# Attention parts made by GpSimd in the loop and five tiles projected in its last slots, in a two-layer transformer kernel

## The reference, cut to what matters

```
ada = silu(c) @ W_ada + b_ada                       # six rows: shift, scale, gate, twice
h = layernorm(x) * (1 + scale_msa) + shift_msa
qkv = h @ W_qkv + b_qkv                             # 16 heads of 18
o = softmax(q k^T / sqrt(18)) v                     # over 1024 tokens of each of 2 sequences
x = x + gate_msa * (o @ W_proj + b_proj)
h = layernorm(x) * (1 + scale_mlp) + shift_mlp
x = x + gate_mlp * (gelu(h @ W_fc1 + b_fc1) @ W_fc2 + b_fc2)
```

## Time and profile before

| what | us |
|---|---|
| median of 3 runs | 917.32 |
| lowest and highest | 916.29, 917.46 |
| the profiled execution | 916.52 |
| its span in the trace | 914.4 |

### The profile page before, as it was taken

One profiled execution on the slowest core, in us unless ns is written; L12 is line 12 of the kernel. 1 busy time (PEld: TensorE's weight loads), 2 busy tenths in 40 slices (PEclk: granted clock), 3 DMA queues, 4 the chain that ended last, 5 costly groups with the idle time before them and its releaser, 6 DMA issues. The chain is left out here.

```text
span 914.4 us, 16701 instructions
## 1 busy us (share of the span) xinstructions
PE 792.0 (87%) x6096; PEld 365.0 (40%) x6096; DVE 649.9 (71%) x1273; ACT 533.5 (58%) x751; POOL 269.9 (30%) x347
## 2 busy tenths in 40 slices
PE   1568989999988989898878899999979875999996
PEld 0334222222222222222215465566646553666564
DVE  4849788888888898989707856646687798844521
ACT  4433576777676777767885636536547634546630
POOL 4320110214463411010005426341223456421122
PEclk9979799999999999999999899999989996999999
DMA  7202000110112110000040011011676720000000
GB/s 227 69 21 72 20 27 27 28 47 20 40 34 59 34 34 14 22 19 20 2 108 0 11 40 41 1 38 44 156 177 163 173 52 16 12 8 27 26 27 27
DMA packets 52127, 45.35 MB, mean 50 GB/s; under 512 B 23898, under 2 KB 41236, under 8 KB 52055
## 3 DMA queue, kind: packets, MB, share of 16 engines
q1 hardware_dynamic: 47613, 36.35, 15.3%
q10 hardware_dynamic: 4442, 8.04, 2.8%
HBM read 27.66 MB, written 9.46 MB: 41 GB/s over the span
## 5 line engine op out<-in xcount | busy, mean ns | idle before, releaser
L921 DVE TENSOR_REDUCE row_max<-ps 128x1 f32<-128x512 f32 x512 | 322.3, 683 | 60.3 <-PE ps L1653 59.4
L1413 ACT ACTIVATE probs<-ps 128x1024 f32<-128x1024 f32 x256 | 248.5, 1018 | 53.9 <-PE ps L1680 53.2
L1653 PE MATMUL ps<-stack_area 54*128 54x512 f16 x512 | 150.2, 388 | 27.1 <-DVE row_max L921 21.8
L1692 PE MATMUL ps<-probs,mlp_area 128*32 128x512 f32 x1024 | 137.2, 608 | 0.4 <-ACT probs L1413 0.4
L1680 PE MATMUL ps<-stack_area 56*128 56x512 f16 x512 | 110.1, 384 | 9.6 <-ACT probs L1413 9.3
L1653 PEld LDWEIGHTS ps<-stack_area 54*128 54x128 f16 x512 | 37.0, 93 | 191.5 <-DVE row_max L921 175.8
L1782 PE MATMUL ps<-mlp_area,w_fc 128*128 128x512 f16 x504 | 110.8, 379 | 1.7 <-issue 0.9
L1803 PE MATMUL ps<-w_fc,mlp_area 128*128 128x288 f16 x864 | 107.7, 286 | 4.6 <-DVE mlp_area L1061 4.6
L1454 ACT ACTIVATE mlp_area<-ps 128x512 f32<-128x512 f32 x72 | 42.9, 595 | 97.7 <-PE ps L1782 95.4
L1803 PEld LDWEIGHTS ps<-w_fc,mlp_area 128*128 128x128 f16 x864 | 83.8, 98 | 27.3 <-DVE mlp_area L1061 3.9
L738 POOL TENSOR_SCALAR neg_scaled<-neg_max 128x16 f32<-128x16 f32 x16 | 4.1, 254 | 292.8 <-DVE neg_max L928 292.8
(11 more groups left out here) (163 smaller groups left out, 1108.7 us busy)
## 6 DMA issues: line engine op xcount, KB each, us to landing
stack_area<-tokens SPq DMA_DIRECT2D x124, 36.0 KB
qkv_rows<-part_area ACTq DMA_DIRECT2D x14, 252.0 KB
qkv_rows<-probs ACTq DMA_DIRECT2D x10, 252.0 KB
x_sb<-in_x SPq DMA_DIRECT2D x4, 576.0 KB, 7.3
w_raw<-in_L_cond_W_fc SPq DMA_DIRECT2D x4, 576.0 KB
tokens<-qkv_rows SPq DMA_DIRECT2D x64, 36.0 KB
v_sb<-qkv_rows SPq DMA_DIRECT2D x16, 144.0 KB
w_raw<-in_L_cond_fc_w SPq DMA_DIRECT2D x4, 576.0 KB
```

Source lines behind the costliest of these rows:

```text
L921: nc.vector.reduce_max(row_max[:, p % 2, t, j, half:half + 1], bank(bk), AX.X).then_inc(max_done, 1)
L1413: nc.scalar.activation(probs[:, n % 2, 2 * c:2 * c + 2, :].rearrange("p h n -> p (h n)"), ps[:, 2 + 2 * c:4 + 2 * c, :].rearrange("p b n - ...
L1653: nc.tensor.matmul(bank(bk), stacks[rows, p % RING, 0, t * P:(t + 1) * P], stacks[rows, p % RING, 1, half * 512:(half + 1) * 512], start=T ...
L1692: mm = nc.tensor.matmul(bank(6)[at:at + VW, :], v_pad[:, TB * (p // BPAIR) + n, 2 * (p % BPAIR) + j, :], probs[:, n % 2, 2 * c + j, :], st ...
```

## The change

- POOL splits the result of each pair in the loop: `normalise_o` writes the pair into one of two float32 buffers (`o_flat`), and `split_attended(p-1)`, which stands behind `split_maxima(p+1)` and ahead of `split_weights`, makes the high part (a float16 copy) and the low part (a subtraction) in `att_parts`, the memory of `v_sb`. The factor 16 is now in the values (`take_v`). The last pair is split by ACT (`last_high`) and DVE (`last_low`) after the loop.
- Tiles 0 to 4 (all of the first sequence) are projected in slots 118 to 127: in an even slot PE turns a tile into bank 0 (`turn_attended`) and DVE copies the columns (`early_columns`), in the next slot PE multiplies into bank 1 (`proj_mms`) and DVE takes the projection. Both PE steps stand between the two halves of `scores`. DVE also makes the statistics of tiles 0 to 2 there. `turn_o` of pair 14 now has bank 7.
- After the loop tiles 5 to 15 follow. Their parts exist already, so that the steps L1442 and L1003 are gone. Tiles 5 to 7 don't need the last pair. The first four MLP tiles are normalised in the steps of tiles 6, 8, 10 and 12, and no longer in the last four.
- POOL's additions and reciprocal roots are unrolled, the roots made for two tiles at once (`invert_two`).
- SP waits for all tiles to be turned, where it waited for the low parts.

```diff
@@ memory
+        att_parts = v_sb[:].rearrange("p t h d -> p t (h d)").bitcast(F16).rearrange("p t (s n) -> p t s n", s=2)
+        o_flat = [tail[:, 2 * L + L // 2 + 2 * C // 2 * i:2 * L + L // 2 + C * (i + 1)] for i in range(2)]
+        freed_cols = tokens[:, 3 * 6 * C:5 * B * L // 2 + 5 * C]
+        hT_att = [freed_cols[:, 320 * i:320 * (i + 1)].bitcast(F16).rearrange("p (k n) -> p k n", k=5) for i in range(2)]
+        y_att = freed_cols[:, 640:640 + 2 * C].rearrange("p (a n) -> p a n", a=2)
@@ constants
+        TAIL_TILES = 5
+        TAIL_FROM = NPAIR * SLOTS - 2 * TAIL_TILES
+        MLP_AT = {6: 0, 8: 1, 10: 2, 12: 3}
@@ SP
-            sp.wait_ge(lo_ready[1], NT)
+            sp.wait_ge(turned[1], NT)
@@ POOL
+            def split_attended(p):
+                pool.wait_ge(o_ready, p + 1)
+                nc.gpsimd.tensor_copy(pair_parts(p, 0), pair_values(p)).then_inc(att_high, 1)
+                pool.wait_ge(att_high, p + 1)
+                nc.gpsimd.tensor_tensor(pair_parts(p, 1), pair_values(p), pair_parts(p, 0), ALU.subtract
+                                        ).then_inc(att_split, 1)
                         if p + 1 < NPAIR:
                             split_maxima(p + 1)
+                        if p:
+                            split_attended(p - 1)
                         if 0 <= p - FIRST_JOB < NJ - QKV_JOBS:
                             split_weights(0, ...)
-                    add_projection(0, 0)
-                    add_projection(0, 1)
-                    with pool.Fori(2, NT) as t:
-                        add_projection(0, t)
-                        invert(t - 2, NT + t - 2)
+                    for t in range(0, NT + 4, 2):
+                        if t < NT:
+                            add_projection(0, t)
+                            add_projection(0, t + 1)
+                        if t > 3:
+                            invert_two(t - 4, NT + t - 4)
@@ DVE, normalise_o
+                if p > 1:
+                    dve.wait_ge(att_split, p - 1)
-                nc.vector.tensor_tensor(v_sb[:, t0:t0 + TB, h:h + 2, 0:D], o[:, :, :, 0:D],
+                nc.vector.tensor_tensor(pair_values(p).rearrange("p t (j d) -> p t j d", j=2), o[:, :, :, 0:D],
@@ DVE, attention, at the end of slot s
+                    if s >= TAIL_FROM:
+                        t, late = divmod(s - TAIL_FROM, 2)
+                        if late:
+                            take_projection(0, t, t % 2, t < 2)
+                        else:
+                            if t > 1:
+                                first_mid_statistics(t - 2)
+                            if t == 0:
+                                dve.wait_ge(late_in, 16 * B)
+                            early_columns(t)
                 normalise_o(NPAIR - 1, 7)
+                last_low()
@@ DVE, after the loop
+                    for t in range(TAIL_TILES, NT + 4):
+                        if 2 <= t < NT + 2:
+                            first_mid_statistics(t - 2)
+                        if t < NT:
+                            take_projection(0, t, t % 2, t < 2)
+                        if t - 1 in MLP_AT:
+                            low_part(2, MLP_AT[t - 1], MLP_AT[t - 1])
+                        if t in MLP_AT:
+                            mlp_normalise(0, MLP_AT[t], MLP_AT[t])
@@ ACT, after the loop
+                    for t in range(TAIL_TILES, NT + 5):
+                        if t == max(2, TAIL_TILES):
+                            last_high()
+                        if t < NT:
+                            take_attended(t)
+                        if t - 3 in MLP_AT:
+                            high_part(2, MLP_AT[t - 3], MLP_AT[t - 3], 0)
+                        if t - 5 in MLP_AT:
+                            i = MLP_AT[t - 5]
+                            take_hT(2, FIRST_BANKS[i], i, h2T[:, :, P * i:P * (i + 1)])
@@ PE, attention, between the halves of scores
+                    if s >= TAIL_FROM:
+                        t, late = divmod(s - TAIL_FROM, 2)
+                        if late:
+                            ...
+                            proj_mms(t, 1, t)
+                        else:
+                            ...
+                            turn_attended(t, 0, t)
@@ PE, after the loop
+                    for t in range(TAIL_TILES, NT + 2):
+                        if t >= TAIL_TILES + 2:
+                            proj_mms(t - 2, 2 + t % 2, t - 3 if t > 3 else 0)
+                        if t < NT:
+                            if t < TAIL_TILES + 2:
+                                pe.wait_ge(proj_y, TAIL_TILES)
+                            turn_attended(t, t % 2, max(0, t - 1))
+                        if t - 4 in MLP_AT:
+                            turn(2, FIRST_BANKS[MLP_AT[t - 4]], MLP_AT[t - 4], True, mlp_hs[MLP_AT[t - 4]])
```

More of the change, by code:

```diff
@@ L1008, in proj_step @@
[L1008 to L1019, removed]
[L1020 to L1029 removed]
+                y = y_sb if l else y_att
@@ new lines, in take_projection, with early_columns, last_low @@
+                nc.vector.scalar_tensor_tensor(y[:, u, :], bank(2 + u if l or t >= TAIL_TILES else 1)[:, 0:C], UN,
+                                               ada[:, t // TB, 2, :], ALU.mult, ALU.mult).then_inc(proj_y, 1)
+            def early_columns(t):
+                dve.wait_ge(turned[1], t + 1)
+                nc.vector.tensor_copy(hT_att[t % 2], bank16(0, F16)[:, 0:5 * P].rearrange("p (k n) -> p k n", k=5)
+                                      ).then_inc(hT_ready[1], 1)
+            def last_low():
+                p = NPAIR - 1
+                dve.wait_ge(att_last, 1)
+                nc.vector.tensor_tensor(pair_parts(p, 1), pair_values(p), pair_parts(p, 0), ALU.subtract
+                                        ).then_inc(att_last, 1)
@@ L1031, in mlp_normalise, with first_mid_statistics @@
+            def first_mid_statistics(t):
+                dve.wait_ge(x_mid, t + 1)
+                statistics(t, NT + t)
             def mlp_normalise(l, t, i):
@@ L1755, in attention, with turn_attended, proj_mms @@
                 turn_o(NPAIR - 1, 7)
-            def proj_mms(l, t, u, first):
-                n = NT * l + t
-                pe.wait_ge(hT_ready[1], n + 1)
-                if not first:
-                    pe.wait_ge(proj_y, n - 1)
+            def turn_attended(t, bk, taken):
+                pe.wait_ge(*attention_split(t))
+                if t >= TB:
+                    pe.wait_ge(att_last, 2)
+                if taken:
+                    pe.wait_ge(hT_ready[1], taken)
+                at = bank16(bk, F16)
+                both = att_parts[:, t]
+                for s in range(2):
+                    for k in range(KB):
+                        blk = KB * s + k
+                        nc.tensor.transpose(at[:, blk * P:(blk + 1) * P], both[:, s, k * P:(k + 1) * P], ident16[:])
+                for i, part in enumerate((both[:, 0, KB * P:C], both[:, 1, KB * P:C], both[:, 0, KB * P:C],
+                                          ones_blk[:])):
+                    mm = nc.tensor.transpose(at[R * i:R * (i + 1), 4 * P:5 * P], part, ident16[:])
+                mm.then_inc(turned[1], 1)
+            def proj_mms(t, bk, taken):
+                pe.wait_ge(hT_ready[1], t + 1)
+                if taken:
+                    pe.wait_ge(proj_y, taken)
                 for i, (a, w) in enumerate(PRODUCTS):
-                    mm = nc.tensor.matmul(bank(2 + u)[:, 0:C], hT[u][:, a, :], w_proj[:, w, :],
+                    mm = nc.tensor.matmul(bank(bk)[:, 0:C], hT_att[t % 2][:, a, :], w_proj[:, w, :],
                                           start=(i == 0), stop=(i == len(PRODUCTS) - 1))
                 mm.then_inc(proj_mm, 1)
-            def proj_step(l, s, u):
-                if not isinstance(s, int) or s > 1:
-                    proj_mms(l, s - 2, u, isinstance(s, int) and s < 4)
-                turn(1, u, NT * l + s, isinstance(s, int) and s < 2)
             def mlp_chunk(l, c, last):
```

100 lines of the change are left out of this document (27 added, 73 removed).

## The result

The changed kernel takes 905.92 us (median of 5 runs, 905.11 to 909.24) against 917.32 (5 runs, 915.94 to 917.51): 0.9892 of the time, with a 95% interval of 0.9869 to 0.9915, so 11.4 us faster. The profiled execution took 905.91 us with a span of 904.1, 10.3 us less than the span of 914.4 before. The forecast was 905.0.

The account below looks back on a forecast made before the run. DVE was taken to bound the loop and the projection, ACT the last slots. L1782 at 503.1 (tail's +2.9 included) instead of 516.63 gives -13.5, plus 1.2 in the loop: -12.3, so 917.3 becomes 905.0 us; range 901 to 911.

Parts of the forecast that it names:

- The step after the loop: Last `weigh` at 478.9 to first fc1 matmul (L1782) at 503.1 instead of 516.63, with DVE bounding after the first takes.
- The loop: Attention loop: POOL's added copy and subtraction per pair cost +1.2 us in all, bounds 0 to 1.6.
- 1.2 us more on POOL is 1.2 us more of waiting: At the loop's one late stack, POOL's added work lengthens PE's 1.17 us wait by 1.2 us.
- at least 2 us early: Attention loop: stacks of the other pairs come this early, as no other such wait is in the loop.
- The tail: Last slots: PE becomes the bound and the last `weigh` comes +2.9 us later, bounds +1.4 to +6.8.
- The fear for `early_columns(2)`: Slot 122: it stands behind statistics waiting for POOL's second addition; ready at 467.6, wanted at 469.2, so nothing lost.
- `early_columns`: Last slots: DVE's copy of 640 columns from PSUM, taken as 0.75 us and covered.
- Contention with POOL: Normalises after the loop: the same 0.5 us each stays; loop reductions reading PSUM don't mind POOL's new work.
- A: Last slots: the tail is serial, PE's inserted work costs 6.8 us instead of 2.9, total 909; chance 0.12.
- B: Loop: POOL's work reaches DVE at every pair, 18 us instead of 1.2, total 921.8; chance 0.05.
- C: New order: PE's clock falls to 1.2 GHz all through, no gain, total 917 to 918; chance 0.04.
- D: Slot 122: DVE waits for POOL and PE behind it, 1 to 2 us more, 906 to 907; in the range.

Follow-up runs that it names:

- e1: Changed kernel with POOL's split of pair p-2 behind `split_part`, instead of pair p-1 ahead of the weights: 905.96 us, ratio to before 0.9877.
- e8: Changed kernel with one more VectorE copy of 288 float32 columns behind each projection take after the loop: span 909.8 us in one execution.
- e3: Changed kernel with `TAIL_TILES = 0`, all 16 tiles projected after the loop: 908.31 us, ratio to before 0.9905.
- e6: Changed kernel with statistics of tiles 3 and 4 ahead of the last pair's `normalise_o`, tile 5's columns ahead of the last high part: 905.93 us, ratio 0.9890.
- e2: Changed kernel with POOL's copy and subtraction of each pair made twice: span 908.8 us in one execution.

## Why the prediction was right, and where its terms were off

The forecast was -12.3 us; the profiled execution shows -10.3 in span, and the medians -11.4. Point by point:

- **The step after the loop was right.** Forecast from the last `weigh` to the first fc1 matmul: 503.1 - 478.9 = 24.2 us; it took 24.04. The normalises cost 1.39 us each (1.5 assumed), the low parts and takes 0.37. No short fall of the clock came in the profiled execution, and e1 shows that it can, for 1.56 us. That this is mostly VectorE's stretch is shown by e8, and limited by e3 and e6: the first two or three tiles go at PE's 1.36 us. The prediction put the last high part ahead of the columns of tile 5 without asking whether it must stand there; e6, which turned the two round and moved two statistics, is 0.7 us shorter.
- **The loop: mechanism right, size off.** The step "1.2 us more on POOL is 1.2 us more of waiting" held (1.17 to 2.34, 3.65 when doubled, 1.17 with POOL's order changed, none with the weight split moved). The term of the sum was 1.2 and measured 2.23: what was missing is that PE, idle for 2.3 us, then runs with a clock of 0.85 and 0.72, and two `weigh` that stood 3.08 us apart stand 4.14 apart. Before, after 1.17 us of waiting, it kept its clock. That the other stacks come "at least 2 us early" did not follow from there being no other wait, which shows only that they come in time; e2, with 2.4 us more on POOL than before and no other such wait, does show it. And DVE alone does not hold the loop by rows 1, where PE is busier (333.94 us against 305.86); nothing in the sum hangs on this.
- **The tail: mechanism right, size off.** The term was +2.9 and measured +4.06. PE became the bound, as forecast, but each half of the scores took 0.32 us instead of 0.27 and the products between them 0.96 instead of 0.87, so that two slots last 4.74 us and not 4.44. From the `weigh` of slot 122 to the last one, forecast as 12.8 us, it took 13.6 (468.73 to 482.32): 0.8 of the missing 1.2 us. The other 0.4 lie in slots 118 to 121, which the prediction had laid out by hand. The fear for `early_columns(2)` was right about the wait and the result: DVE waited for POOL 1.1 us (until 470.08), PE not at all, with 0.8 us to spare, which e2 used up.
- **`early_columns`** takes 0.49 us for 640 columns from PSUM, less than the 0.75 assumed; it was covered either way.
- **Contention with POOL.** It stayed in the new order, as forecast, but smaller: in the changed kernel the second operation of each normalise takes 0.85 us instead of 0.52, so 0.33 us each and not 0.5. The Trainium skill (GPSIMD Engine Reference, section 8, Key points) names VectorE instructions with two SBUF inputs as those that contend. L927 and L937 have two and double in e8, and the reductions of the loop, which read PSUM, kept 0.68 us on average with 18 us more work on POOL (e2), so the runs agree.
- **Rivals.** A, a serial tail of +6.8, did not come: 4.06 of it, as the first tiles hide. B falls by e1 and e2. C, the slow clock all through, did not come; by its own terms (L1782 at 518.2) it would have been 918.9 us and not 917 to 918. D cost nothing, and e2 shows the same wait at 0.5 us.

So the median came within 0.9 us of the forecast, while the profiled execution shows 2.0 us less gain than forecast, all of it in the loop and the tail. That the median lies closer than the trace is luck: two terms were too small by 1.0 and 1.2 us, and the stages that the sum does not touch vary by as much between executions. The up to 1.4 us of low clock in the trace of before is in no term of the sum either.

What stays open: why the clock falls after the loop in one execution and not in another with the same PE work (e1 against the changed kernel), how often it does so before and after, and the loss of 0.3 us between pairs 10 and 11 in e2.

## What to carry to other kernels

Work given to an idle engine costs what stands behind it in that engine's queue: follow its order to the first transfer with no margin, and put the new work behind that one. When an engine becomes the bound by inserted work, take the price of each group at the place where it will stand, since groups that used to run back to back are broken. An idle gap on PE like the 2.34 us here is to be priced with the slower matmuls behind it, 1.06 us in this loop. And an experiment that sets a constant changes everything that is derived from it: read where every step stands before its result is put down to one of them.

## What the runs showed of the hardware that was not expected

- A PE wait of 1.17 us in the loop left the granted clock at 1.00; waits of 2.34 and 3.65 us were followed by 0.85 then 0.72, and by 0.98 then 0.59, in the windows 284 to 288 and 288 to 292. The first cost 1.1 us beyond the longer wait (interval + 2.23 for + 1.17 of waiting); doubling the wait again cost 0.2 beyond it (+ 1.48 for + 1.31).
- Two score matmuls of 56 rows followed by a full-height matmul take 0.32 us by starts, four in a row 0.54: parting the four in two costs PE 0.10 us. The seven products take 0.09 us more ahead of scores than ahead of transposes (0.96 against 0.87), and as much ahead of the last `weigh` (481.36 to 482.32).
- In e8 a VectorE operation with two SBUF inputs that started within 0.06 us behind a GpSimd addition took 1.05 us instead of 0.45, so an edit that only shifts it can cost 0.6 us. Where VectorE had started first, the addition took longer: 0.94 us in the changed kernel (at 492.26, behind L936 at 492.09) against 0.79 (at 488.33, beside VectorE's statistics, which have one input in SBUF).
